# First expert layer of an attention and expert stack on rows sorted by expert

## The chip, the cores and the metric

The kernel runs on one core of a Trainium2 chip. The metric is the device time of one execution in microseconds (us). TensorE (PE) multiplies matrices; VectorE (DVE), ScalarE (ACT) and GpSimd (POOL) work on tiles in on-chip memory; SyncE (SP) issues transfers, and POOL issues the indirect ones, whose rows are named by a list. Each engine runs its own queue in order, and semaphores tie them together. TensorE runs at one of two clock levels, 1.2 or 2.4 GHz.

## What is computed

A residual stack of four pairs: attention over a context, then an expert layer (FFN), on x of 4 batches x 512 rows x 128 features. The change touches the first expert layer:

```python
gate_logits = x @ Wg + bg                                # x: 2048 rows, 8 experts
top_vals, top_idx = jax.lax.top_k(gate_logits, 2)
w = jax.nn.softmax(top_vals, axis=-1)
combine = jnp.sum(one_hot(top_idx, 8) * w[..., None], axis=-2)
h = jnp.einsum('td,edh->eth', xf, W0) + b0[:, None, :]    # 128 -> 512
g = silu(jnp.einsum('td,edh->eth', xf, W1) + b1[:, None, :])
y = jnp.einsum('eth,ehd->etd', h * g, W2) + b2[:, None, :]
out = jnp.einsum('te,etd->td', combine, y)
```

Two of the eight gates of a row are not zero. The second expert layer (one expert a row, with a capacity of 321 rows each) is computed in the kernel before on gathered rows already; the third and fourth (two experts a row) on all rows.

## The kernel before

Rows are held in four blocks of 512 (one batch each, B = 4), each of four tiles of 128 (TB = 4). x_tok has rows on partitions, xnT is the normalised x with features on partitions. Each engine has a hand-written program, `for s in range(N_SUB)`, over the eight sub-layers; the order in it is the order of the engine.

Sub-layer 0 is attention0. DVE's part of it calls replicate_columns, which waits until all of wP and woP (weights of the second attention, in_l1) have been loaded; SP issues these loads one after another behind its first loads. Then finish(0, b) adds the result of block b to x_tok, statistics and scale normalise it, and TensorE transposes the block.

Sub-layer 1 is ffn(0). It runs over expert e and block b, unit k = 4 e + b. hidden (TensorE) makes, for each of four chunks c of 128 hidden features, the products with W1 and W0 over 512 rows, and down the product with W2. A product is made of three matmuls (lines 2084 to 2086): weights and data are split into a high and a low part, in a format that needs one pass each, and high x high, high x low and low x high are summed. POOL makes the splits of the weights (w_p), ACT and DVE those of the hidden rows (h_p). ACT applies silu (gS), DVE multiplies with the other product (h_f), and sums y with the gate of each row, replicated over partitions through memory (gate_d, wrep). The result is summed in acc, transposed and added to x_tok by finish(1, b); the layer norm for the second attention follows, with key preparations (prep1) between.

POOL's before_heads(1), memsets and small splits for the second attention, stood behind that layer since its tiles share memory with it. routed() is the second expert layer: its products (lines 2569 and 2580) are single matmuls in fp32, and POOL stores and loads rows by indirect transfers (lines 802 and 809).

## Time and profile before

| | us |
|---|---|
| median of 3 runs (1529.68 to 1534.11) | 1530.49 |
| the profiled execution | 1535.88 |
| its span, first to last instruction | 1534.1 |
| mean granted clock of TensorE | 0.931 |
| busy: TensorE, DVE, ACT, POOL | 1333, 1115, 879, 685 |

The profile is of one execution. A row of the timeline has the start, the duration, the engine, the line of the kernel, the tiles written and read with their shapes, how many instructions are merged in it, and in brackets how long the engine was idle before it and what ended that. The page's tenths are shares of 40 equal slices of 38.4 us. TensorE's durations overlap; the time from start to start is what counts. An fp32 matmul appears as two instructions.

### The profile page before, as it was taken

Reading aid. Unit: us, or ns where it says so; the run is one execution under the profiler, and the core shown is the slowest. Engines: PE = TensorE matmul, PEld = TensorE weight load, DVE = VectorE, ACT = ScalarE, POOL = GpSimd, SP = SyncE. Lnnn points to the kernel's source line nnn. Section 1 sums busy time; section 2 is a strip of 40 time slices with the busy share of each in tenths; the row PEclk is TensorE's granted clock in tenths of the full one; section 3 lists DMA queues with packets and bytes.
Section 4 is the critical chain, followed back from the end, with each engine's and each line's share of the span. In section 5 each row is a group of like instructions: output and inputs, shape, how many; then the busy total and the mean of one; then the engine's idle time right before and its main releaser. Section 6 shows DMA issues by size and latency. Waiting matters only on the chain.

```text
span 1534.1 us, 23669 instructions
## 1 busy us (share of the span) xinstructions
PE 1333.4 (87%) x7106; PEld 975.5 (64%) x7106; DVE 1114.5 (73%) x2762; ACT 878.9 (57%) x2592; POOL 684.6 (45%) x1144
## 2 busy tenths in 40 slices
PE   4595989999967889779199999879789999998998
PEld 4432767888854555468177776556577776676886
DVE  4047778888887887842676667889866676788987
ACT  1001656556537889524187787534467878665664
POOL 2002322223025666434465556446355557545652
PEclk9657999999989999969599999999989999999999
DMA  3500014111042000222100000042101000014110
GB/s 79 21 22 0 22 38 150 55 49 35 1 50 62 1 2 2 58 81 70 48 12 18 1 2 8 5 148 97 34 15 43 1 2 14 1 29 144 62 56 28
DMA packets 85021, 60.17 MB, mean 39 GB/s; under 512 B 29779, under 2 KB 67691, under 8 KB 84896
## 3 DMA queue, kind: packets, MB, share of 16 engines
q1 hardware_dynamic: 83488, 55.97, 14.1%
q0 software_dynamic: 1408, 2.70, 0.6%
q8 instruction: 58, 0.95, 0.3%
q14 instruction: 67, 0.55, 0.1%
HBM read 52.38 MB, written 6.27 MB: 38 GB/s over the span
## 4 chain that ended last, share of the span: by engine, by line
PE 57%; DVE 17%; issue 6%; ACT 5%; POOL 4%; DMA 2%; SPq 0%; DVEq 0%; ACTq 0%; POOLq 0%
PE ps L2084 13%; PE ps L2085 12%; PE ps L2086 12%; PE ps L2221 5%; PE ps L2235 4%; DVE h_p L1753 4%; PE ps L2249 2%; ACT ex L1184 2%; DVE xn_tok L1383 2%; DVE acc L1772 1%; PE ps L2580 1%; PE ps L2569 1%; POOL pp L883 1%; DVE ln_st L1369 1%; PE ps L2170 1%
## 5 line engine op out<-in xcount | busy, mean ns | idle before, releaser
L883 POOL TENSOR_TENSOR pp<-ex,rc 128x256 f32<-128x256 f32 x384 | 235.8, 614 | 216.5 <-DVE rc L1799 155.0
L1753 DVE TENSOR_TENSOR h_p<-h_f,h_p 128x512 fp32r<-128x512 f32 x320 | 259.8, 835 | 29.1 <-POOL h_p L696 24.3
L1039 ACT ACTIVATE ex<-ps,nmx 128x154 f32<-128x154 f32 x512 | 194.3, 389 | 74.9 <-DVE nmx L1794 73.4
L1794 DVE TENSOR_REDUCE nmx<-ps 128x2 f32<-128x308 f32 x256 | 120.1, 471 | 93.1 <-PE ps L2086 92.9
L2084 PE MATMUL ps<-q_s,w_p 128*128 128x512 f32 x448 | 180.5, 403 | 7.5 <-DVE h_f L1978 3.0
L2086 PE MATMUL ps<-q_s,w_p 128*128 128x512 f32 x448 | 177.8, 397 | 0.0
L2085 PE MATMUL ps<-q_s,w_p 128*128 128x512 f32 x448 | 177.8, 397 | 0.0
L2084 PE MATMUL ps<-h_p,w_p 128*128 128x512 f32 x320 | 131.3, 410 | 14.4 <-DVE h_p L1753 12.9
L967 ACT ACTIVATE gS<-ps,biasT 128x512 f32<-128x512 f32 x128 | 88.2, 690 | 88.0 <-PE ps L2086 88.0
L696 POOL CAST h_p<-h_f 128x512 fp32r<-128x512 f32 x96 | 80.9, 843 | 118.3 <-ACT h_f L977 117.9
L1978 DVE SCALAR_TENSOR_TENSOR h_f<-ps,biasT,gS 128x512 f32<-128x512 f32 x128 | 95.6, 749 | 48.6 <-ACT gS L967 30.4
L2085 PE MATMUL ps<-h_p,w_p 128*128 128x512 f32 x320 | 127.5, 398 | 0.0
L2086 PE MATMUL ps<-h_p,w_p 128*128 128x512 f32 x320 | 126.9, 396 | 0.0
L654 POOL TENSOR_TENSOR ln_r<-ln_v,mhalf 128x4 f32<-128x4 f32 x36 | 38.2, 1062 | 195.4 <-DVE ln_v L1374 195.3
L674 POOL TENSOR_TENSOR w_p<-w_s,ones 128x512 fp32r<-128x512 f32 (+1 forms) x56 | 59.4, 1084 | 144.2 <-PE ps L2086 143.4
L2221 PEld LDWEIGHTS ps<-ident,pp 128*128 128x128 f32 x640 | 73.6, 141 | 59.8 <-POOL pp L884 34.2
L1184 ACT ACTIVATE ex<-ps,nmx 128x154 f32<-128x154 f32 x256 | 97.8, 394 | 20.5 <-DVE nmx L1647 20.1
L2084 PEld LDWEIGHTS ps<-q_s,w_p 128*128 128x128 f32 x448 | 84.8, 189 | 33.5 <-DVE h_f L1978 5.5
L884 POOL TENSOR_TENSOR pp<-ex,rc 128x52 f32<-128x52 f32 x384 | 105.1, 274 | 0.0
L2221 PE MATMUL ps<-ident,pp 128*128 128x128 f32 x640 | 99.5, 279 | 4.6 <-POOL pp L884 4.6
L1039 ACT ACTIVATION_READ_ACCUMULATOR ex<-ps,nmx 128x1 f32 x512 | 103.0, 201 | 0.0
L2084 PE MATMUL ps<-kp,q_s 128*128 128x308 f32 x256 | 95.7, 374 | 6.1 <-ACT ex L1039 6.1
(313 smaller groups left out, 3339.9 us busy)
## 6 DMA issues: line engine op xcount, KB each, us to landing
w_s<-in_L_ffn_W SPq DMA_DIRECT2D x48, 256.0 KB, 4.1
wrep<-gate_d SPq DMA_DIRECT2D x48, 256.0 KB, 3.5
xnT<-gate_d SPq DMA_DIRECT2D x48, 256.0 KB, 4.2
w_e<-in_L_ffn_W SPq DMA_DIRECT2D x8, 256.0 KB, 4.8
...
```

The source lines that it names most:

```text
L883: pool.tensor_tensor(pp[st % 2][:, m % 4, 2 * j:2 * j + 2, :], w[:, :, 0:P], r.broadcast_to([P, 2, P]), ALU.mult)
L884: pool.tensor_tensor(pp[st % 2][:, m % 4, 4, :].rearrange("p (h c) -> p h c", h=4)[:, 2 * j:2 * j + 2, 0:SK - P], w[:, :, P:SK], r.broadca ...
L967: act.activation(gS[c % 2][:, :], ps[:, c % 2, :], f["act"], **bias).then_inc(f_a, 1)
L1039: ins = act.activation(ex[:, tt % NEX, j, :], ps[:, tt % 3, j * SK:(j + 1) * SK], ACT.Exp, bias=nmx8[:, tt % 8, j:j + 1], accum_out=sm8[:, ...
L1184: ins = act.activation(ex[:, tt % NEX, j, :], ps[:, tt % 3, j * SK:(j + 1) * SK], ACT.Exp, bias=nmx8[:, tt % 8, j:j + 1], accum_out=sm8[:, ...
L1753: dve.tensor_tensor(lo[:, c, :], h_f[:, (n * k + c) % NHF, :], hi[:, c, :].bitcast(F32), ALU.subtract).then_inc(f_hl, 1)
L1794: dve.tensor_reduce(nmx8[:, tt % 8, :], ps[:, tt % 3, 0:2 * SK].rearrange("p (h s) -> p h s", h=2), AX.X, ALU.max, negate=True).then_inc(n ...
L1978: dve.scalar_tensor_tensor(out=h_f[:, (n * k + c) % NHF, :], in0=ps[:, 2 + c % 2, :], scalar=biasT[:, 32 + e * n + c:33 + e * n + c], in1= ...
L2084: mm(bank, w[0], x[0], start=first, stop=False)
L2085: mm(bank, w[0], x[1], start=False, stop=False)
L2086: return mm(bank, w[1], x[0], start=False, stop=last)
L2221: last = pe.transpose(ps[:, bank, k * P:(k + 1) * P], pp[st % 2][:, k, c, :], ident[:, :])
```

## The change

The first expert layer is no longer computed for all rows and experts. sorted_runs(), a program for each engine, does this:

1. TensorE computes the gate logits (choices), DVE picks the two experts of each row (choose), and triangular products (rank) give each of the 4096 choices its place among those of its expert (ranks).
2. runs_of_experts gives each expert whole runs of 256 places; (4096 + 8 x 255) / 256 gives 23 runs, always all computed. DVE (contents) and ACT (places) make two tables for each block, and 32 matmuls (lists) of them give, for each place of each run, the source row src_i, the row dst_i for its result, and its gate w_r.
3. For each run k: POOL gathers 2 x 128 rows of the normalised x from memory (xr_d); TensorE transposes them (columns), ACT copies them (xc_r). SP reads the run's expert from a table in on-chip memory (value_load) and loads its W1, W0 and W2 (three buffers). hidden_run makes 8 products of 256 columns, in fp32, ACT the silu with the expert's bias, DVE the product (products), down_run 8 products of 128 columns, DVE multiplies with the gate (weigh), and POOL scatters the rows into yr_d, one half for a row's first choice, one for its second, places without a row behind both.
4. The bias b2 comes from four matmuls with the gates (turn, bias_out) in runs 1 to 5. When the last scatters have landed, SP loads both halves of yr_d into acc and y_second, and finish(1, b) adds both.

before_heads(1) now stands on POOL behind the first four gathers. Its place and the tables' sit in memory that the splits used; the splits, gate replication and sums of this layer are gone. The stores that fill xs_d and y_d for the second expert layer come behind the loads of yr_d. Layers 2 to 4 keep their computation.

```diff
-    DENSE = (0, 2, 3)
-    CNT = (0, 1, 1, 2, 3)
+    DENSE = (2, 3)
+    CNT = (0, 0, 0, 1, 2)
+    SPARSE = 0
+    HALVES = 2
+    RUN = HALVES * P
+    NRUN = (2 * B * S + E * (RUN - 1)) // RUN
+    NCOL = NRUN * HALVES
+    NXG, NW = 4, 3
...
+            sp.dma_start(b1_rows[:, :], t["L0_ffn_b1"]).then_inc(in_l1, 16)
+            sp.dma_start(b0_rows[:, :], t["L0_ffn_b0"]).then_inc(in_l1, 16)
+            sp.wait_ge(const_g, 4)
+            for k in range(TB):
+                sp.dma_start(b2_blk[k * E:(k + 1) * E, k * D:(k + 1) * D], t["L0_ffn_b2"]).then_inc(in_l1, 16)
...
+                def first_weights(k):
+                    u = k % NW
+                    e = sp.value_load(expert_i[0:1, k:k + 1], min_val=0, max_val=E - 1)
+                    wait(sp, s_h, 2 * (k - NW + 1))
+                    sp.dma_start(w1_r[u][:, :], t[f["w1"]][bass.ds(e, 1)].rearrange("a p h -> p (a h)")).then_inc(s_wr[u], 16)
+                    sp.dma_start(w0_r[u][:, :], t[f["w0"]][bass.ds(e, 1)].rearrange("a p h -> p (a h)")).then_inc(s_wr[u], 16)
+                    return e
+                def last_weights(k, e):
+                    u = k % NW
+                    wait(sp, s_yp, k - NW + 1)
+                    sp.dma_start(w2_r[u][:, :, :], t[f["w2"]][bass.ds(e, 1)].rearrange("a (c p) d -> p (a c) d", p=P)).then_inc(s_wr[u], 16)
+                for b in range(B):
+                    sp.wait_ge(ln_ok, B * ln_index(1) + b + 1)
+                    sp.dma_start(xr_d[b * S:(b + 1) * S, :].rearrange("(k p) d -> p k d", p=P), xn_tok[:, tiles(b), :]).then_inc(s_xd, 16)
+                sp.wait_ge(*by_v("expert"))
+                for k in range(NRUN):
+                    e = first_weights(k)
+                    last_weights(k, e)
+                for u in range(2):
+                    sp.wait_ge(s_out[u], 16 * HALVES * ((NRUN + 1 - u) // 2))
+                for b in range(B):
+                    for c, into in enumerate((acc, y_second)):
+                        sp.dma_start(into[:, bsl(b)].rearrange("p (k d) -> p k d", k=TB),
+                                     yr_d[c * B * S + b * S:c * B * S + (b + 1) * S, :].rearrange("(k p) d -> p k d", p=P)).then_inc(y_in[b], 16)
...
-            dense(0)
+            sorted_runs()
...
+                def gather(k):
+                    wait(pool, s_xp, k - NXG + 1)
+                    for h in range(HALVES):
+                        c = k * HALVES + h
+                        pool.indirect_dma_start(xr[k % NXG][:, h, :], None, xr_d[:, :], bass.IndirectOffsetOnAxis(ap=src_i[:, c:c + 1], axis=0)).then_inc(s_xr[k % NXG], 16)
+                def scatter(k):
+                    pool.wait_ge(s_y, k + 1)
+                    for h in range(HALVES):
+                        c = k * HALVES + h
+                        pool.indirect_dma_start(yr_d[:, :], bass.IndirectOffsetOnAxis(ap=dst_i[:, c:c + 1], axis=0), yr[k % 2][:, h, :], None).then_inc(s_out[k % 2], 16)
+                pool.wait_ge(*by_v("ids"))
+                pool.wait_ge(s_xd, 16 * B)
+                for k in range(NXG):
+                    gather(k)
+                before_heads(1)
+                for k in range(NRUN):
+                    scatter(k)
+                    if k + NXG < NRUN:
+                        gather(k + NXG)
...
+                act.preload_act_table(FFN[SPARSE]["act"])
+                act.wait_ge(*by_p("bias"))
+                act.activation(bias_r[:, :, :], ps[:, 7, 0:8 * NRUN].rearrange("p (c k) -> p c k", c=8), ACT.Identity).then_inc(s_a, 1)
+                act.wait_ge(*by_a("bias"))
+                columns(0)
+                columns(1)
+                for k in range(NRUN):
+                    gates(k, 0)
+                    gates(k, 1)
+                    if k + 2 < NRUN:
+                        columns(k + 2)
+                    if 1 <= k <= B:
+                        turned(k - 1)
...
+                    dve.wait_ge(y_in[b], 32)
+                    link(dve.tensor_tensor(x_tok[:, tiles(b), :], x_tok[:, tiles(b), :], y_second[:, bsl(b)].rearrange("p (n d) -> p n d", n=TB), ALU.add))
+                    more = acc[:, bsl(b)]
...
+                def contents(b):
+                    def over_cols(ap):
+                        return ap.rearrange("p (n a) -> p n a", a=1)
+                    into = what[b // 2][:, b % 2, :, :]
+                    link(dve.tensor_tensor(same[:, :, :], col_of[:, :].rearrange("p (a k) -> p a k", a=1).broadcast_to([P, 2 * TB, NCOL]),
+                                           over_cols(first[:, b, :]).broadcast_to([P, 2 * TB, NCOL]), ALU.is_equal))
+                    for c in range(2):
+                        dve.tensor_tensor(into[:, c * TB:(c + 1) * TB, NCOL:2 * NCOL], same[:, c * TB:(c + 1) * TB, :], over_cols(r_w[:, c, tiles(b)]).broadcast_to([P, TB, NCOL]), ALU.mult)
+                    link(dve.tensor_tensor(into[:, :, 0:NCOL], same[:, :, :], over_cols(val[:, b, :]).broadcast_to([P, 2 * TB, NCOL]), ALU.mult))
+                    dve.sem_inc(s_v, 1)
...
+                def products(k, q):
+                    G = 2 * k + q
+                    dve.wait_ge(s_ga, G + 1)
+                    dve.wait_ge(s_h, G + 1)
+                    wait(dve, s_yp, k - 1)
+                    for c in range(2):
+                        ins = dve.scalar_tensor_tensor(out=h_r[k % 2][:, 2 * q + c, :], in0=ps[:, 2 + G % 2, c * RUN:(c + 1) * RUN], scalar=bias_r[:, 4 + 2 * q + c, k:k + 1],
+                                                       in1=g_r[G % 2][:, c, :], op0=ALU.add, op1=ALU.mult)
+                    ins.then_inc(s_hd, 1)
+                def weigh(k):
+                    dve.wait_ge(s_yp, k + 1)
+                    wait(dve, s_out[k % 2], 16 * HALVES * (k // 2))
+                    for h in range(HALVES):
+                        ins = dve.tensor_scalar(yr[k % 2][:, h, :], ps[:, 5, h * D:(h + 1) * D], w_r[:, HALVES * k + h:HALVES * k + h + 1], None, ALU.mult)
+                    ins.then_inc(s_y, 1)
+                def add_bias(b):
+                    dve.wait_ge(*by_p("b2", b))
+                    dve.tensor_tensor(x_tok[:, tiles(b), :], x_tok[:, tiles(b), :], ps[:, 7, :].rearrange("p (n d) -> p n d", n=TB), ALU.add).then_inc(s_v, 1)
...
+                def hidden_run(k):
+                    pe.wait_ge(s_wr[k % NW], 48 * (k // NW + 1))
+                    pe.wait_ge(s_x, k + 1)
+                    for q in range(2):
+                        G = 2 * k + q
+                        wait(pe, s_ga, G - 1)
+                        for c in range(2):
+                            last = mm(ps[:, G % 2, c * RUN:(c + 1) * RUN], w1_r[k % NW][:, (2 * q + c) * P:(2 * q + c + 1) * P], xc_r[k % 2][:, :], start=True, stop=True)
+                        last.then_inc(s_g, 1)
+                        wait(pe, s_hd, G - 1)
+                        for c in range(2):
+                            last = mm(ps[:, 2 + G % 2, c * RUN:(c + 1) * RUN], w0_r[k % NW][:, (2 * q + c) * P:(2 * q + c + 1) * P], xc_r[k % 2][:, :], start=True, stop=True)
+                        last.then_inc(s_h, 1)
+                def down_run(k):
+                    pe.wait_ge(s_hd, 2 * k + 2)
+                    wait(pe, s_y, k)
+                    for h in range(HALVES):
+                        for c in range(4):
+                            last = mm(ps[:, 5, h * D:(h + 1) * D], h_r[k % 2][:, c, h * P:(h + 1) * P], w2_r[k % NW][:, c, :], start=(c == 0), stop=(c == 3))
+                    last.then_inc(s_yp, 1)
...
+                hidden_run(0)
+                for k in range(NRUN):
+                    if k + 1 < NRUN:
+                        hidden_run(k + 1)
+                    if k + 2 < NRUN:
+                        columns(k + 2)
+                    down_run(k)
+                    if 1 <= k <= B:
+                        turn(k - 1)
+                    if 2 <= k < 2 + B:
+                        bias_out(k - 2)
```

The order of TensorE at the start of the layer, before: transposes of attention 0's result (acc) and of the normalised x (xn_tok), then the split matmuls; w_p_67, w_p_68 are the parts of W1, w_p_75, w_p_76 those of W0, q_s holds those of x.

```order
L2053 MATMUL ps<-ident,acc 128x128 x16
L2040 MATMUL ps<-ident,xn_tok 128x128 x16
L2084 MATMUL ps<-q_s,w_p_67 128x512
L2085 MATMUL ps<-q_s,w_p_67 128x512
L2086 MATMUL ps<-q_s,w_p_68 128x512
L2084 MATMUL ps<-q_s,w_p_75 128x512
L2085 MATMUL ps<-q_s,w_p_75 128x512
L2086 MATMUL ps<-q_s,w_p_76 128x512
```

Six matmuls make one pair of hidden products there, and they start right behind the transposes.

TensorE now, from the count of choices per expert (total) on: biases, the first half of the lists, then the columns of runs 0 and 1 (xr), the hidden products of run 0, and further down columns(2) and down_run(0).

```order
L3140 MATMUL ps<-total,ones 128x8
L3076 MATMUL ps<-expert_oh,b_rows 128x23 x8
L3067 MATMUL ps<-what_177,where 128x92 x16
...
L3084 MATMUL ps<-ident,xr_148 128x128 x2
L3084 MATMUL ps<-ident,xr_149 128x128 x2
L3095 MATMUL ps<-xc_r_167,w_r_154 128x256 x2
L3099 MATMUL ps<-xc_r_167,w_r_157 128x256 x2
...
L3084 MATMUL ps<-ident,xr_150 128x128 x2
L3108 MATMUL ps<-w_r_160,h_r_163 128x128 x8
```

Between the transposes and the first product stand the gate logits, ranks, biases and lists; the columns of a run stand two runs ahead of it, behind the hidden products of the next run.

POOL before, behind the layer norms' ln_r: the splits of the first expert's weights (w_s) and of x.

```order
L654 TENSOR_TENSOR ln_r<-ln_v,mhalf 128x4 x8
L674 TENSOR_TENSOR w_p_67<-w_s,ones 128x512
L674 TENSOR_TENSOR w_p_71<-w_s,ones 128x512
L674 TENSOR_TENSOR w_p_75<-w_s_79,ones 128x512
L681 TENSOR_TENSOR w_p_68<-w_s,w_p_67 128x512
L681 TENSOR_TENSOR w_p_72<-w_s,w_p_71 128x512
L681 TENSOR_TENSOR w_p_76<-w_s_79,w_p_75 128x512
L704 TENSOR_TENSOR q_s<-xnT,q_s 128x512 x4
```

These splits are gone from POOL.

POOL now: gathers of four runs, before_heads (its last op is the memset of wkT), then scatter and gather in turn.

```order
L778 TENSOR_TENSOR ln_r<-ln_v,mhalf 128x4 x8
L909 DMA xr_148<-xr_d,src_i 128x128 x2
L909 DMA xr_149<-xr_d,src_i 128x128 x2
...
L909 DMA xr_151<-xr_d,src_i 128x128 x2
L985 MEMSET kz_111 128x2464
L986 MEMSET pp_104 128x4x128
...
L1001 MEMSET wkT_99 128x512
L916 DMA yr_d<-yr_152,dst_i 9984x128 x2
L909 DMA xr_148<-xr_d,src_i 128x128 x2
L916 DMA yr_d<-yr_153,dst_i 9984x128 x2
L909 DMA xr_149<-xr_d,src_i 128x128 x2
```

The gather of run k + 4 stands behind the scatter of run k, and before_heads ahead of the first scatter.

SP at the start of the program, before: biases and mask, then the weights of the second attention, and the first expert's weights.

```order
L498 DMA bias_rows<-in_L_ffn_b 32x128 x4
L499 DMA mask_i<-in_mask_Bx1xSxS_if 128x16x154
L505 DMA wP<-in_L_xattn_Wq 8x8x1 x16
L505 DMA wP<-in_L_xattn_Wk 8x8x1 x16
L505 DMA wP<-in_L_xattn_Wv 8x8x1 x16
L509 DMA woP<-in_L_xattn_Wo 8x128x1 x16
L540 DMA w_s<-in_L_ffn_W 128x512
```

The loads of w_s went at this place with their addresses fixed.

SP now, the same place, and then the start of sorted_runs: stores of the normalised rows, the read of the expert of run 0, and its first two loads (the third, of W2, follows).

```order
L580 DMA mask_i<-in_mask_Bx1xSxS_if 128x16x154
L582 DMA b_rows<-in_L_ffn_b 8x512
L583 DMA b_rows<-in_L_ffn_b 8x512
L586 DMA b_blk<-in_L_ffn_b 8x128 x4
L591 DMA wP<-in_L_xattn_Wq 8x8x1 x16
...
L595 DMA woP<-in_L_xattn_Wo 8x128x1 x16
L682 DMA xr_d<-xn_tok 128x4x128 x4
L668 TENSOR_LOAD expert_i
L668 ISA x2
L670 ISA
L670 DMA w_r_154<-in_L_ffn_W 128x512
L671 DMA w_r_157<-in_L_ffn_W 128x512
```

Six loads stand ahead of wP and woP, and the loads of expert weights stand behind a read of expert_i.

## Rows read from the trace of the kernel before

**Rows 1.** The page, parts 1 and 2: busy time, and clock in 40 slices.

```profile
PE 1333.4 (87%) x7106; PEld 975.5 (64%) x7106; DVE 1114.5 (73%) x2762; ACT 878.9 (57%) x2592; POOL 684.6 (45%) x1144
...
PEclk9657999999989999969599999999989999999999
```

**Rows 2.** Windows: length, busy of PE, PEld, DVE, ACT, POOL, clock, DMA, GB/s.

```profile
154.70:440.30 285.60, 277.95 (x1192) 222.53 (x1192) 234.79 (x401) 165.12 (x270) 65.96 (x49) 0.98 0.15 47
```

**Rows 3.** Timeline, TensorE: start, duration, line; the layer's first matmuls and late ones.

```profile
154.69 0.77 PE L2084 MATMUL ps<-q_s,w_p 128*128 128x512 f32 x1 [2.72 <-ACT q_s L914]
...
158.67 0.52 PE L2084 MATMUL ps<-q_s,w_p 128*128 128x512 f32 x1
...
430.65 0.39 PE L2085 MATMUL ps<-q_s,w_p 128*128 128x512 f32 x1
430.88 0.39 PE L2086 MATMUL ps<-q_s,w_p 128*128 128x512 f32 x1
```

**Rows 4.** Timeline, TensorE in the middle (fp32) expert layer.

```profile
691.71 2.87 PE L2580 MATMUL ps<-w_s,h_s 128*128 128x128 f32 x24
694.42 2.33 PE L2569 MATMUL ps<-xs,w_e 128*128 128x321 f32 x8
696.58 0.44 PE L2557 MATMUL ps<-ident,xg 128*128 128x128 f32 x3
696.86 2.87 PE L2580 MATMUL ps<-w_s,h_s 128*128 128x128 f32 x24
```

**Rows 5.** Timeline, ACT in the same layer: four activations of 321 columns.

```profile
697.40 1.78 ACT L1245 ACTIVATE h_s<-ps,biasT 128x321 f32<-128x321 f32 x4
```

**Rows 6.** Timeline, DVE and POOL at that layer's end: PSUM operand, indirect stores.

```profile
727.86 0.42 DVE L1600 TENSOR_TENSOR y_s<-ps,b2rep 128x256 f32<-128x256 f32 x1 [1.38 <-PE ps L2580]
728.04 0.96 POOL L809 DMA_INDIRECT y_d<-y_s,xg  x1 [0.30 <-issue]
...
729.31 0.91 POOL L809 DMA_INDIRECT y_d<-y_s,xg  x1 [0.30 <-issue]
...
733.08 0.92 POOL L809 DMA_INDIRECT y_d<-y_s,xg  x1 [0.30 <-issue]
```

**Rows 7.** DMA issues: count, KB each, median us from issue to landing.

```profile
w_e<-in_L_ffn_W SPq DMA_DIRECT2D x8, 256.0 KB, 4.8
...
y_d<-y_s,xg POOLq DMA_INDIRECT x24, 2.2
```

**Rows 8.** DMA rate in 40 slices of the stretch 686 to 706 us.

```profile
GB/s 286 272 307 327 312 343 337 341 335 328 338 257 71 5 0 0 0 0 0 119 217 359 311 174 0 0 131 0 94 94 135 338 330 222 46 19 131 0 46 21
```

**Rows 9.** Chain of work: start, duration, four 128x8 products of the gate (x8).

```profile
654.38 1.86 PE ps L2537 x8
```

**Rows 10.** Timeline, DVE: first and last op of the choice for one block.

```profile
648.06 0.18 DVE L1555 COPY lg<-ps 128x32 f32<-128x32 f32 x1
...
650.13 0.17 DVE L1572 TENSOR_TENSOR cum<-cum,oh_sum 128x8 f32<-128x8 f32 x1
```

**Rows 11.** Timeline, DVE: scaling of block 3 before the first expert layer.

```profile
146.49 4.31 DVE L1383 TENSOR_SCALAR xn_tok<-x_tok,ln_mv,ln_r 128x128 f32<-128x128 f32 x4 [0.20 <-POOL ln_r L654]
```

**Rows 12.** Timeline, SP's loads at the start, and DVE behind the last.

```profile
11.46 1.70 SPq L498 DMA_DIRECT2D bias_rows<-in_L_ffn_b  x4
...
34.49 35.98 SPq L509 DMA_DIRECT2D woP<-in_L_xattn_Wo  x16
...
76.22 0.90 DVE L1450 COPY wP<-wP 128x128 f32<-128x128 f32 x6 [32.26 <-DMA woP<-in_L_xattn_Wo]
```

**Rows 13.** Timeline, DVE behind the first and behind the middle expert layer.

```profile
440.27 0.68 DVE L1414 TENSOR_TENSOR x_tok<-x_tok,ps 128x512 f32<-128x512 f32 x1
...
445.71 2.17 DVE L1624 SCALAR_TENSOR_TENSOR kz<-kz_hi,neg_lo,ps 32x308 fp32r<-32x308 f32 x4 [3.12 <-POOL pp L846]
...
461.48 1.11 DVE L1383 TENSOR_SCALAR xn_tok<-x_tok,ln_mv,ln_r 128x128 f32<-128x128 f32 x4
...
738.25 0.69 DVE L1414 TENSOR_TENSOR x_tok<-x_tok,acc 128x512 f32<-128x512 f32 x1 [9.11 <-DMA acc<-y_d]
```

554 lines of the change are left out of this document (379 added, 175 removed).

## The prediction

> **What bounds the kernel now.** I read first the page's busy line and clock row [rows 1]: TensorE is busy 87% of the span, mostly at full clock. Then the stretch from the first matmul of the first expert layer, at 154.7 us, to its end at 440.3 us, when the sum of row block 0 is added to x_tok [rows 2, 3, 13]. In these 285.6 us TensorE is busy 278 us. The layer makes 8 experts x 4 row blocks x 36 matmuls = 1152 (12 hidden products, three matmuls each), one every 0.235 us at full clock [rows 3], 271 us. So TensorE bounds this stage, and every row goes through all eight experts although two of them have a weight. A cut of its work pays, until another chain ends later.
>
> **Removed.** These 285.6 us. The splits of weights and x on POOL, the replication of gates and the sums of y go too; they lay beside TensorE and count nothing.
>
> **Added 1: SP's queue at the start.** Six loads (two of b1_rows and b0_rows, four of b2_blk) stand ahead of the loads of wP and woP. SP issues small loads 0.43 us each, about 0.47 us apart [rows 12], and the woP loads end at 70.5 us. DVE waited 32.3 us for just those, and the chain of attention 0 waits for DVE behind it [rows 12]. So all that follows is later by 6 x 0.47 = 2.8 us.
>
> **Added 2: routing.** I walked DVE and TensorE through the new order from 134.4 us on (x_tok of block 0; this part stands as before). Prices: a group of 128x8 products, four matmuls, takes TensorE 1.86 us at the low clock of that stretch, 0.46 us a matmul [rows 1, 9]. What choose(b) does for one block on DVE took 2.2 us, with some ten small ops about 0.2 us apart [rows 10]; it now has three more ops, so 2.6 us. ranks(b) is six small ops, 1.4 us. TensorE has, per block, choices(b) 1.9 us and rank(b), five matmuls, 2.3 us, in one line with the transposes of the next block, which wait for DVE. So the two engines wait for each other in turn:
> - choose(0) 146.1 to 148.7, scale of block 2 to 152.0, transposes, rank(0) and choices(1) on TensorE to 157.2 (DVE idles 5 us), choose(1) to 159.9, scale of block 3 and ranks(0) to 162.5, choose(2) after choices(2), 166.4 to 169.0, choose(3) to 173.0, ranks(3) to 177.1.
> - runs_of_experts, 14 small ops, to 180.6, shares to 180.9. contents(b): 368 elements take about 0.54 us, half of them 0.35 us (estimates from the 128x256 op at 0.42 us [rows 6] and the small ones [rows 10]), so 0.54 + 2 x 0.35 + 0.54 with gaps 1.95 us, four times: 188.7.
> - The list matmuls follow DVE; those of the last block take 2 us if the clock has risen by then (biases and lists keep TensorE busy from 179 on), up to 3.7 us if not: 190.7. dst_i and src_i: 191.2.
> - POOL issues two gathers 1.27 us apart [rows 6] per run, and PE turns runs 0 and 1 before the first product: the fourth gather starts at 195.1 and lands 2.2 us later [rows 7]. First hidden product at 198, against 154.7: **43.3 us**. The expert weights are asked for from 179 on, 19 us ahead, and cost nothing here; ACT's squares end about 181.
>
> **Added 3: 23 runs.** Of these products the fp32 layer in the middle of the kernel has rows: four matmuls of 321 columns from start to start 2.16 us, so 0.54 us each, linear in columns (0.43 us for 256); twelve of 128 columns 2.71 us, 0.226 us each; three transposes 0.28 us [rows 4]. A run has 8 of 256 columns (3.45), 8 of 128 (1.81), 2 transposes (0.19): 5.45 us, 23 of them 125.3 us, less 0.4 us for the two transposes counted above. ACT: one copy and four 128x256 gates, 0.39 us each from 0.445 at 321 [rows 5], 2.0 us. DVE: four ops at 0.42 us and two smaller, 2.3 us. POOL: two scatters, two gathers, 5.05 us [rows 6]. None exceeds TensorE alone, but POOL is close.
> - In the four runs with turn(b) and bias_out(b), ACT waits at turned(b) for a transpose behind down_run, and its next gates come 1.2 us late; bias_out has 512 columns, 0.87 us; with the turn 2.2 us a run, **8.9 us**.
> - TensorE idles before the first run, so the first 4 us run at half clock, as at 154.7 where nine matmuls took 4.0 us instead of 2.1 [rows 3]: 2 us.
> - The ring of rows: columns(k) turned, hidden products, weigh about 3.75 us after columns(k+2), two scatters and one gather ahead (3 x 1.27), second gather landing after L, transposes 0.2. This closes over two runs: period = 3.9 + L/2. TensorE's 5.45 holds up to L = 3.1 us. The bounds for L are the 2.2 us of a scatter and the 4.8 us of a 256 KB load beside others [rows 7]. I take the middle, 3.5 us, since a gather reads from memory while loads run: 5.65 us, 0.20 x 23 = **5 us**.
> - w2 of run k is issued after down_run(k-3): period = (5.45 + landing)/2, 5.1 us with 4.8 us for the landing [rows 7]; slack.
> - Bytes: 768 KB of weights and 256 KB of rows a run; at the 330 GB/s that the busiest slices moved [rows 8] 3.2 us of 5.65.
>
> Sum: 124.9 + 8.9 + 2 + 5 = **141 us**.
>
> **Added 4: the way back.** weigh 0.5, second scatter 1.3 behind the first. In the middle layer the first x_tok addition came 5.2 us after the last scatter began [rows 6, 13]; here block 0 needs two loads: 5.7. **7.5 us**. What follows (layer norm, key preparations) took DVE 22.3 us to 462.6 with 3.1 us of waiting for POOL's memsets [rows 13]. These now stand after gather(3), hidden behind runs 0 and 1 (5.3 us to the last memset); four second additions of 0.72 us take their place: 0.2 us less, taken as 0. If their cover is gone, 5.3 us.
>
> **Sum.** 285.6 - 43.3 - 141 - 7.5 - 2.8 = 91 us. The profiled execution had a span of 1534.1 and a time of 1535.9, so 1445 on its scale; it lies 5.4 us above the median of 1530.5, and against the median it is **1439 us**. Layers behind are unchanged; their initial stores of xs_d and y_d slide with the layer and have the whole of attention 1.
>
> **A rule against this change.** The row: DVE's four scalings of block 3 took 4.31 us [rows 11] while POOL split weights, where the same four take 1.11 beside an idle POOL [rows 13]; so the two do block each other. POOL's indirect stores beside DVE's ops on PSUM took 0.96 us and alone 0.92 [rows 6]. The Trainium skill, SBUF — State Buffer, "SBUF: two separate sides", says that transfers issued by GpSimd starve while VectorE holds the shared port, 620 ns becoming about 3100. By that rule the four of a run would take some 12 us and the kernel would lose; by the row they don't. The same rule spares VectorE ops with a PSUM operand, and all in the runs have one: by that rule, the trace agrees.
>
> **Rivals.**
> - *A transfer chain sets the run.* L near 4.8 us gives 6.3 us, or w2's landing stretched to 7 us by the other two loads and the rows gives 6.2; for it speaks that all four kinds of transfer run at once, and that the layer has only three weight buffers; against it the 3.2 of 5.65 us. 0.6 x 23 = 14 us more: 1453.
> - *Routing longer.* If the clock stays low and each small op costs 0.05 us more (some 120 in a row), 10 us more: 1449.
> - *Slower than before: POOL's issue.* If DVE holds back each indirect transfer, the period is four issues. From 2.4 us each (9.6 us a run = 5.65 + 91/23) nothing is gained; with the factor 3.9 of [rows 11] on 1.27 us it is 4.9 us, 19.6 us a run, +320 us: about 1760. Against it [rows 6].
> - *It doesn't do what it says.* The number of runs is fixed at 23 and nothing is skipped; were all fp32 products double the rows' price, +120 us, 1559. [Rows 4] exclude it nearly.
>
> **How the numbers follow.** Forecast 60%, transfer chain 22%, routing longer 13%, POOL's issue 3%, price of products 1%, something between 1%. Low end: period 5.45 (-5) and routing 12 us shorter, if DVE and TensorE interleave better: 1422. High end: transfer chain and routing longer, 1439 + 14 + 10 + 3 for the memsets: 1466. About 0.3% is what a measurement of this kernel can tell from no change. Faster 0.95, same 0.01, slower 0.04.
>
> **What would show it.** TensorE's first 256-column product about 201 us (2.8 us shift in it), start to start of runs 5.4 to 5.7 us late in the stage, PE busy over 90% there, the granted clock full; about 347 us for the first addition of y_second. Wrong: idle TensorE before the transposes with the gather as releaser (ring), before the first product of a run with a weight load as releaser (w2), POOL's indirect rows over 2 us, or a routing over 50 us.

## The result, and the profile after

The changed kernel takes **1438.2 us** (median of 4 runs, 1434.3 to 1441.4) against 1530.1 us (4 runs, 1529.5 to 1534.1): ratio 0.939, 95% interval 0.936 to 0.942. The forecast was 1439. The profiled execution took 1436.3 us, its span 1434.6. Busy times and clock row of its page, to be read beside [rows 1]:

```profile
PE 1225.5 (85%) x6850; PEld 903.5 (63%) x6850; DVE 957.1 (67%) x2652; ACT 772.0 (54%) x2480; POOL 701.7 (49%) x1189
PEclk9667579997799996886999999999899999999999
```

108 us of TensorE's busy time are gone. In slice 5 (143 to 179 us) the clock row has 5: there the routing lies. Next come two windows, the end of the routing and the 23 runs, with the columns of [rows 2]:

```profile
160.00:193.00 33.00, 21.80 (x99) 20.93 (x98) 15.31 (x67) 12.36 (x30) 4.99 (x5) 0.50 0.26 80
193.70:334.00 140.30, 134.89 (x793) 116.78 (x793) 52.28 (x141) 44.60 (x119) 89.90 (x96) 0.99 0.51 152
```

In the runs TensorE is busy 134.9 of 140.3 us at full clock, and the transfer engines half the time. The layer is still bound by TensorE. The next rows are the marks on DVE that end each stage, to be read beside [rows 12] and [rows 13]: the copy behind the woP loads, the addition of block 0 to x_tok, the list of places, the last weigh, the first addition of y_second, the last scale:

```profile
69.12 0.90 DVE L1633 COPY wP<-wP 128x128 f32<-128x128 f32 x6 [24.63 <-DMA woP<-in_L_xattn_Wo]
125.27 0.69 DVE L1597 TENSOR_TENSOR x_tok<-x_tok,ps 128x512 f32<-128x512 f32 x1 [4.28 <-PE ps L2378]
185.80 0.20 DVE L2249 TENSOR_TENSOR dst_i<-ps,spare_r 128x46 int32<-128x46 f32 x1 [8.82 <-PE ps L3067]
333.89 0.61 DVE L2276 TENSOR_SCALAR yr<-ps,w_r 128x128 f32<-128x128 f32 x2 [2.21 <-PE ps L3108]
342.19 0.69 DVE L1589 TENSOR_TENSOR x_tok<-x_tok,y_second 128x512 f32<-128x512 f32 x1 [7.69 <-DMA y_second<-yr_d]
363.01 1.11 DVE L1562 TENSOR_SCALAR xn_tok<-x_tok,ln_mv,ln_r 128x128 f32<-128x128 f32 x4
```

TensorE's timeline between them: the biases, the lists, the first two transposes, the first hidden products.

```profile
168.28 3.57 PE L3076 MATMUL ps<-expert_oh,b_rows 8*128 8x23 f32 x16 [3.21 <-DVE expert_oh L2216]
171.83 13.93 PE L3067 MATMUL ps<-what,where 128*128 128x92 f32 x64
190.61 0.69 PE L3084 MATMUL ps<-ident,xr 128*128 128x128 f32 x2 [4.84 <-DMA xr<-xr_d,src_i]
193.18 0.69 PE L3084 MATMUL ps<-ident,xr 128*128 128x128 f32 x2 [1.89 <-DMA xr<-xr_d,src_i]
193.66 1.91 PE L3095 MATMUL ps<-xc_r,w_r 128*128 128x256 f32 x4
195.37 1.91 PE L3099 MATMUL ps<-xc_r,w_r 128*128 128x256 f32 x4
197.08 1.11 PE L3095 MATMUL ps<-xc_r,w_r 128*128 128x256 f32 x4
```

Both traces, stage by stage, beside the prediction:

| stage | before, us | after, us | predicted |
|---|---|---|---|
| first addition to x_tok | 134.42 | 125.27 | 137.2 |
| from there to the first hidden product (before: of the old layer) | 20.3 | 68.4 | 63.6 |
| the layer itself; the 23 runs to the last weigh | 285.6 | 140.2 | 141 |
| last weigh to the first addition of y_second | | 8.3 | 7.5 |
| from the layer's first addition to the end of the span | 1093.8 | 1092.4 | same |

The right end holds to 0.1%, but three terms do not: the start came 9.2 us earlier where 2.8 later was forecast, the routing is 4.8 us longer, and 0.8 us change sides between runs and way back. Against the profile of before the forecast was 1445 and the profiled run took 1436.3; against the median the difference is 0.8 us. The experiments ask what lies behind the start, the runs, the routing and the covers.

### The profile page after: what moved, and what is told of

It is laid out like the page before. It is cut to its first block, busy times and chain, and to the rows that moved or that the text cites. A ratio compares the mean times of both kernels' runs of the same rounds, so it can differ in the third digit from the quotient of the medians.

```text
span 1434.6 us, 23042 instructions
## 1 busy us (share of the span) xinstructions
PE 1225.5 (85%) x6850; PEld 903.5 (63%) x6850; DVE 957.1 (67%) x2652; ACT 772.0 (54%) x2480; POOL 701.7 (49%) x1189
## 4 chain that ended last, share of the span: by engine, by line
PE 55%; DVE 18%; issue 9%; POOL 5%; DMA 5%; ACT 5%; SPq 4%; DVEq 0%; ACTq 0%; POOLq 0%
PE ps L2409 8%; PE ps L2411 7%; PE ps L2410 7%; PE ps L2533 5%; PE ps L2547 4%; DVE h_p L1933 3%; PE ps L2561 2%; DMA xr<-xr_d,src_i 2%; PE ps L3108 2%; SPq L595 2%; DVE xn_tok L1562 2%; ACT ex L1310 2%; PE ps L3095 2%; DVE ln_st L1548 2%; PE ps L2879 1%
## 5 line engine op out<-in xcount | busy, mean ns | idle before, releaser
L1933 DVE TENSOR_TENSOR h_p<-h_f,h_p 128x512 fp32r<-128x512 f32 x192 | 160.5, 871 | 25.4 <-POOL h_p L819 22.8
L2409 PE MATMUL ps<-kp,q_s 128*128 128x308 f32 x256 | 94.8, 370 | 6.6 <-ACT ex L1165 6.6
L2267 DVE SCALAR_TENSOR_TENSOR h_r<-ps,bias_r,g_r 128x256 f32<-128x256 f32 x92 | 38.3, 477 | 91.6 <-ACT g_r L1466 81.2
L2409 PE MATMUL ps<-h_p,w_p 128*128 128x512 f32 x192 | 80.2, 418 | 14.5 <-DVE h_p L1933 12.8
L1106 ACT ACTIVATE h_f<-ps,biasT 128x512 f32<-128x512 f32 x128 | 82.0, 695 | 9.4 <-DVE h_p L1933 9.4
L2365 PE MATMUL ps<-ident,xn_tok 128*128 128x128 f32 x80 | 20.9, 412 | 69.3 <-DVE xn_tok L1562 68.9
L2409 PE MATMUL ps<-q_s,w_p 128*128 128x512 f32 x192 | 77.4, 403 | 1.6 <-POOL q_s L824 1.5
L2411 PE MATMUL ps<-kp,q_s 128*128 128x308 f32 x256 | 78.7, 308 | 0.0
L2410 PE MATMUL ps<-kp,q_s 128*128 128x308 f32 x256 | 78.7, 307 | 0.0
L2410 PE MATMUL ps<-h_p,w_p 128*128 128x512 f32 x192 | 76.6, 399 | 0.0
L2411 PE MATMUL ps<-h_p,w_p 128*128 128x512 f32 x192 | 76.3, 397 | 0.0
L2411 PE MATMUL ps<-q_s,w_p 128*128 128x512 f32 x192 | 76.2, 397 | 0.0
```

Source lines behind the costliest of these rows:

```text
L1106: act.activation(h_f[:, (n * k + c) % NHF, :], bank, f["act"], **bias).then_inc(f_a, 1)
L1933: dve.tensor_tensor(lo[:, c, :], h_f[:, (n * k + c) % NHF, :], hi[:, c, :].bitcast(F32), ALU.subtract).then_inc(f_hl, 1)
L2409: mm(bank, w[0], x[0], start=first, stop=False)
L2410: mm(bank, w[0], x[1], start=False, stop=False)
L2411: return mm(bank, w[1], x[0], start=False, stop=last)
```

## Experiments

The ratio and its 95% interval are against the kernel before, run on the same chip. The intervals of the changed kernels overlap in most cases, so a difference of a few us between two of them is called shown only where a trace shows it too.

**The six loads at the start.** One kernel changes the changed kernel, two the kernel before.

```diff
# loads_apart: the loads of b1_rows, b0_rows, b2_blk behind those of woP
-            sp.dma_start(b1_rows[:, :], t["L0_ffn_b1"]).then_inc(in_l1, 16)
...
+            sp.dma_start(b1_rows[:, :], t["L0_ffn_b1"]).then_inc(in_b, 16)
...
-                pe.wait_ge(in_l1, 16 * (3 * HEADS + 16 + 2 + TB))
+                pe.wait_ge(in_b, 16 * (2 + TB))
```

> The changed kernel, with the six loads of b1, b0 and b2 issued behind the loads of woP, on a semaphore of their own that only the bias products wait for. Theory of the prediction (each load ahead costs its issue, 0.47 us): 2.8 us faster than the changed kernel. Rival, from the traces (x_tok of block 0 came 9.1 us earlier in the changed kernel although six loads stand ahead): the six loads ahead are what made the strided loads behind them go faster; then this kernel is slower by about 6 us than the changed one.

Measured: 1442.0 us (1434.3 to 1445.8), ratio 0.939 (0.935 to 0.944). The interval holds that of the changed kernel, so neither 2.8 us less nor 6 us more is shown.

```diff
# b_six: the kernel before with six such loads ahead of those of wP
+            sp.dma_start(pt_s[0][0:E, :], t["L0_ffn_b1"]).then_inc(in_l1, 16)
+            sp.dma_start(pt_s[1][0:E, :], t["L0_ffn_b0"]).then_inc(in_l1, 16)
+            for k in range(TB):
+                sp.dma_start(pt_s[2][k * E:(k + 1) * E, k * D:(k + 1) * D], t["L0_ffn_b2"]).then_inc(in_l1, 16)
...
```

> The kernel before, with the six loads of the changed kernel added at the same place of SyncE's queue, into tiles that are free then. Theory of the prediction: 2.8 us slower than before. Rival (their place shifts the strided loads onto a faster pattern, 29.6 instead of 36.0 us for woP): 3 to 7 us faster than before. Third possibility: the strided loads vary from execution to execution by themselves; then neither sign is clear of the spread.

Measured: 1531.1 us (1526.2 to 1539.4, 10 runs), ratio 0.999 (0.997 to 1.001).

```diff
# b_experts_wait: the kernel before, loads of expert weights wait for those of woP
+            sp.wait_ge(in_l1, 16 * (3 * HEADS + 16))
```

> The kernel before, with SyncE waiting until all loads of wP and woP have landed before it issues the first expert loads. Theory (in the kernel before, 1.5 MB of expert loads right behind woP delayed its landing: 5.8 us from the last issue to VectorE's start, 4.0 us in the changed kernel): VectorE starts about 1.7 us earlier and the kernel is 1 to 2 us faster; the expert weights arrive 6 us later and are still in time. Rival (the difference lies in the issue of the strided loads alone): no change.

Measured: 1534.1 us (1523.7 to 1542.4, 10 runs), ratio 1.001 (0.997 to 1.005).

SP's rows of the woP loads (start, duration of the issue) in the traces of the kernel after, loads_apart, b_experts_wait and b_six, in this order:

```profile
35.48 29.60 SPq L595 DMA_DIRECT2D woP<-in_L_xattn_Wo  x16
```
```profile
35.05 33.97 SPq L591 DMA_DIRECT2D woP<-in_L_xattn_Wo  x16
```
```profile
34.23 39.26 SPq L509 DMA_DIRECT2D woP<-in_L_xattn_Wo  x16
```
```profile
34.74 30.48 SPq L513 DMA_DIRECT2D woP<-in_L_xattn_Wo  x16
```

The same 16 loads take 29.6 to 39.3 us in these traces, and 36.0 in that of the kernel before [rows 12]. Over all fourteen kernels of this document, ten of the eleven with six loads ahead took 29.1 to 31.0 us and one (loads_twice) 36.6; the three without took 34.0, 36.0 and 39.3. But in the times of ten runs b_six differs from the kernel before by 0.1%, and its interval leaves room for 4.6 us gained or 2.1 us lost, not for the 2.8 us of the prediction. In b_experts_wait DVE still starts 5.3 us behind the last issue (5.8 in the kernel before), so the expert loads were not what made the woP loads land late. Of the 9 us between the starts of the kernels before and after, the six loads can have given at most those 4.6; the rest is, as far as the runs show, a difference of two executions. Whether six loads ahead shorten the issue stays open: the traces lean to it, the times do not show it.

**Gathers first.** The ring of rows was a term of the sum (5 us): the gather of run k + 4 waits on POOL behind the two scatters of run k, and TensorE meets its rows two runs later.

```diff
                 for k in range(NRUN):
-                    scatter(k)
                     if k + NXG < NRUN:
                         gather(k + NXG)
+                    scatter(k)
```

> The changed kernel with one edit on GpSimd: the gather of run k+4 is issued ahead of the scatter of run k. Theory (ring of rows: period 3.9 + L/2 with the two scatters in it): the gather then waits only for its buffer, which is free a run earlier; all transposes find their rows, every run takes 5.45 us instead of the 5.7 us measured late in the stage, and the time falls by 4 to 6 us. Rival (weight loads, or memory traffic as such, stretch the runs): the idle time before the transposes moves to the first hidden product of a run and the time falls by less than 1.5 us.

Measured: 1434.8 us (1433.5 to 1438.2), ratio 0.936 (0.933 to 0.939). In the kernel after the late transposes wait for their rows, first block; with the gathers first they don't, second block (TensorE, one late run each):

```profile
269.93 1.03 PE L3099 MATMUL ps<-xc_r,w_r 128*128 128x256 f32 x4
271.56 0.44 PE L3084 MATMUL ps<-ident,xr 128*128 128x128 f32 x2 [0.61 <-DMA xr<-xr_d,src_i]
271.83 1.95 PE L3108 MATMUL ps<-w_r,h_r 128*128 128x128 f32 x16
```
```profile
276.22 1.03 PE L3099 MATMUL ps<-xc_r,w_r 128*128 128x256 f32 x4
277.09 0.38 PE L3084 MATMUL ps<-ident,xr 128*128 128x128 f32 x2
277.31 1.95 PE L3108 MATMUL ps<-w_r,h_r 128*128 128x128 f32 x16
```

Thirteen late runs (down_run to down_run, from the eighth on) take 5.46 us each where the kernel after has 5.46 to 6.59, 5.81 in the mean. 5.46 is TensorE's own time, forecast as 5.45. The gathers still land after 3.0 us (median from 215 to 320 us), but they are asked for a run earlier. From the first to the last down_run it is 124.5 us against 129.3: the ring cost 4.8 us, forecast 5. The medians differ by 3.4 us, but the intervals of the two ratios overlap; the trace shows it, the times only agree.

**Who stretches the gathers, and how much room the transfers have.** loads_small (the kernel after) and loads_twice (gathers first):

```diff
# loads_small: from run 3 on a sliver of each weight
+                    n = 4 * P if k < NW else 16
-                    sp.dma_start(w1_r[u][:, :], t[f["w1"]][bass.ds(e, 1)].rearrange("a p h -> p (a h)")).then_inc(s_wr[u], 16)
+                    sp.dma_start(w1_r[u][:, 0:n], t[f["w1"]][bass.ds(e, 1), :, 0:n].rearrange("a p h -> p (a h)")).then_inc(s_wr[u], 16)
...
# loads_twice: each weight once more, into tiles that are free in these runs
+                    for w1_to, w0_to in ((w1_r[u], w0_r[u]), (more_r[u][0], more_r[u][1])):
...
-                    pe.wait_ge(s_wr[k % NW], 48 * (k // NW + 1))
+                    pe.wait_ge(s_wr[k % NW], 96 * (k // NW + 1))
```

> The changed kernel, except that from run 3 on each load of an expert's weights brings only a sliver (64 bytes a partition, some 24 KB a run in place of 768 KB); the products are then made with the weights of runs 0 to 2 that lie in the buffers, so the sum of the layer is another one. It asks whether the traffic of the weights sets the landing of the gathers and with it the period of the runs. In the changed kernel 13 late runs took 5.81 us each, the gathers landed after 3.0 us (median) and the transposes waited for them. Theory A (the ring of rows is made of POOL's order and of POOL's issue, 1.29 us each): the landing falls to 2.2 to 2.6 us, but the period stays between 5.6 and 5.8 us; time 0 to 4 us less than the changed kernel's 1438. Theory B (the weights' transfers stretch the gathers): the landing falls to about 2.2 us and all late runs take 5.46 us, TensorE's own time; 7 to 8 us less, about 1430. Theory C (the wait is for the weights themselves): the period falls to 5.46 and the landing of the gathers stays at 3.0.

> The kernel with the gathers issued ahead of the scatters (runs 5.46 us each, set by TensorE, 1434.8 us), with every weight load of the 23 runs issued a second time into tiles that are free then; hidden_run waits for all six. A run then moves 1536 KB of weights and 256 KB of rows instead of 1024 KB. It prices the slack of the transfers. My theory, after the prediction's account (3.2 of 5.65 us are needed at 330 GB/s; period by w2's ring (5.45 + landing)/2): 1.79 MB at 330 GB/s are 5.4 us, just at TensorE's 5.46, and landings grow to 5 to 7 us, so a run takes 5.5 to 6.2 us: 0 to 17 us more, middle 1442. Rival (the transfer chain was close to being the bound already): a run takes 7 us or more, +35 us, 1470. Other rival (the transfers have far more slack than the bytes say): 5.46 us as before, 1435, and the slices of the stage show over 330 GB/s.

Measured: loads_small 1434.2 us (1431.5 to 1437.4), ratio 0.938 (0.934 to 0.941); loads_twice 1439.0 us (1435.7 to 1442.8), ratio 0.940 (0.936 to 0.943). DMA part of the traces from 215 to 320 us, busy tenths, rates, then the issues with count, KB each and median us to landing; loads_small first:

```profile
DMA packets 9845, 5.39 MB, mean 51 GB/s; under 512 B 8690, under 2 KB 8690, under 8 KB 9836
xr<-xr_d,src_i POOLq DMA_INDIRECT x36, 2.5
```
```profile
DMA  9999797995985899999999999999999999999999
DMA packets 31164, 32.75 MB, mean 312 GB/s; under 512 B 2850, under 2 KB 20867, under 8 KB 31155
more_r<-in_L_ffn_W SPq DMA_DIRECT2D x54, 256.0 KB, 4.5
xr<-xr_d,src_i POOLq DMA_INDIRECT x36, 4.2
```

The kernel after shows 3.0 us there. With slivers the gathers land in 2.5 us and the late runs take 5.47 us although POOL's order is the old one: theory B, though its 7 to 8 us was too much. From the first to the last down_run it is 124.5 us against 129.3, as with the gathers first, and the median is 4.0 us lower. So the old order costs time only where the weights' traffic delays the gathers. The Trainium skill (DMA: Bandwidth & Descriptors, Anatomy of one DMA — SWDGE (gpsimd) path) gives a transfer of 64 KB issued by GpSimd about 2.15 us, an estimate from its formula; the trace comes near it only with the other traffic nearly gone, and beside it measures 3.0 and 4.2. With the doubled loads the transfer engines are busy 96% at 312 GB/s and the gathers take 4.2 us, and still the late runs take 5.52: gathers issued a run earlier have the room for that. So TensorE stays the bound at 1.75 times the bytes, which agrees with the prediction's account (3.2 of 5.65 us). From first hidden product to last down_run it is 0.6 us more than with single loads; the other 3.6 us of the median are not shown by this stage, and the intervals overlap.

**Run size.** This kernel has the gathers first too.

```diff
-    HALVES = 2
+    HALVES = 1
```

> The kernel with the gathers issued ahead of the scatters, with runs of 128 rows: 39 runs in place of 23 (4992 rows computed in place of 5888). By TensorE a run then takes 8 x 0.226 for the hidden products, 4 x 0.226 for W2 and 0.09 for the transpose, 2.8 us; 39 of them 109 us, against 125.6. But each run loads its 768 KB of weights, and 128 KB move in and out. Theory A (my account of the transfers): 896 KB at 330 GB/s are 2.7 us, just below TensorE, but the ring of w2 gives (2.8 + landing) / 2 with a landing of 4.5 us, as in the kernel with doubled loads, so 3.6 us a run: 142 us, 14 us more than now (1449), with TensorE waiting for weights. Rival B (TensorE stays the bound): 2.8 us a run, 16 us less: 1419. Rival C (POOL's issue, two transfers of 1.29 us a run, or SP's three loads with the reading of the expert's number): 2.6 us, below TensorE, unless SP takes over 0.9 us a load.

Measured: 1440.6 us (1436.2 to 1445.3), ratio 0.943 (0.937 to 0.949). TensorE's waits of the stretch, and one of them in its timeline:

```profile
PE ps L3095 <- DMA w_r<-in_L_ffn_W: 13.1, 17, 1.5
PE ps L3095 <- ACT g_r L1466: 1.4, 2, 0.9
```
```profile
244.82 0.71 PE L3095 MATMUL ps<-xc_r,w_r 128*128 128x128 f32 x4 [0.85 <-DMA w_r<-in_L_ffn_W]
```

A run takes 3.24 us where nothing waits, not 2.8: the four products with W2 take 1.14 us until the next run starts instead of 0.90, and each of the first two pairs of hidden products 0.50 to 0.55 instead of 0.45. That each now waits for a neighbour which 256 columns had covered is likely, but not shown. Thirteen late runs take 3.65 us in the mean, since the weights come late 17 times in the 39 runs, 13.1 us in all. From the first hidden product to the last down_run it is 141.5 us against 133.7: what the 15% fewer rows save is more than lost. That is theory A, whose 142 us was right. Its "14 us more" was not, since it counted from 125.6 us, the bare price of 23 runs, and not from the 133.7 that they take with their biases and the first run's clock; the median is 5.8 us above that of the kernel with the gathers first.

**The cover of the memsets.**

```diff
-                before_heads(1)
                 for k in range(NRUN):
...
                     scatter(k)
+                before_heads(1)
```

> The kernel with the gathers ahead of the scatters, and before_heads(1) on POOL moved from behind the first four gathers to behind the last scatter, its cover gone. The prediction said: 5.3 us if that cover is gone. Theory A (as the prediction): +5.3 us, 1440. Theory B (from the trace of the kernel with the gathers first): POOL's last scatter is issued at 334.2 and its next work, the first reciprocal root of the layer norm, comes at 342.3; the memsets take 7.4 us (198.3 to 205.6) and end at 341.6, before anything waits for them: +0 to 1 us, 1435. And the second run may start up to 1 us earlier, since scatter 0 and gather 4 no longer stand behind the memsets.

Measured: 1436.4 us (1434.0 to 1439.8), ratio 0.939 (0.935 to 0.943). POOL, last memset:

```profile
339.96 0.97 POOL L1001 MEMSET wkT<- 128x512 f32 x2
```

They run from 332.9 to 340.9 us. DVE waits for the rows of yr_d until 338.1, and POOL is needed next at 341.2, for the layer norm, so they end just in time; the first addition of y_second comes 8.3 us behind the last weigh in both kernels and the last scale 20.9 us behind that (20.8 with the memsets early). Theory B: it costs nothing, and the prediction's "if their cover is gone, 5.3 us" was wrong. The way back is itself a cover, with 0.3 us to spare.

**The clock of the lists.** Two sizes of one edit; the results of the matmuls added are read by nobody.

```diff
# warm, with the gathers first; lists_mixed has also the last two lines
+                spin(16)
                 biases()
                 lists()
+                spin(22)
                 columns(0)
+                spin(8)
                 columns(1)
...
+                    for _ in range(n):
+                        mm(ps[:, 3, 0:256], ident_bf[:, :], ident[:, :].bitcast(BF16), start=True, stop=True)
...
+                            if b < 2:
+                                mm(ps[:, 3, 0:256], ident_bf[:, :], ident[:, :].bitcast(BF16), start=True, stop=True)
```

> The kernel with the gathers ahead of the scatters, with matmuls that nobody reads (256 columns, bf16) in TensorE's idle time: 16 before the biases (3.2 us idle there), 22 between lists and the first transposes (4.75 us idle), 8 between the transposes of runs 0 and 1 (1.8 us idle). It asks what the low clock of the lists and of the first run costs. There the 64 instructions of the lists took 13.93 us at the low clock, although TensorE had been busy without a gap for 17.5 us by their end; the first products of 256 columns ran 3.4 us at the low clock. Theory A (activity ahead raises the clock and the small matmuls keep it): lists take about 7 to 8 us, the first hidden product comes 5 to 6 us earlier, and the first run gains 1.7 us: 7 us less than 1434.8, 1428. Theory B (the wide matmuls raise the clock, the narrow ones of the lists let it fall again or keep it low): lists about 14 us still, the first run at full clock: 1.7 us less, 1433. Theory C (no effect at all, the clock stays low until 197): 1435.

> The kernel with matmuls that nobody reads in TensorE's idle time (before the biases, behind the lists, between the first transposes; there the lists still took 13.96 us at the low clock, and the clock rose 2 us into the matmuls behind them), and 16 more of them among the lists, one of 256 columns behind each of the first 16 of the 32 products. At the low clock one costs 0.22 us (3.57 us for 16). Theory A (it is the narrow fp32 products that keep the clock low, wide ones between them raise it): the granted clock rises within the lists; up to the rise the stretch takes some 0.65 us for a product and a wide one, then half, and lists and wide ones end after about 11 us, 3 us before; 1429. Theory B (they don't raise it): lists take 13.9 + 3.5 = 17.4 us, 3.5 us more than the kernel without, and the first hidden product comes 3.5 us later: about 1436 against 1432.

Measured: warm 1432.3 us (1429.2 to 1438.0), ratio 0.937 (0.933 to 0.941); lists_mixed 1429.3 us (1422.7 to 1434.2), ratio 0.935 (0.930 to 0.941). TensorE in warm, then in lists_mixed (its rows in the lists alternate, four stand for them):

```profile
162.34 3.57 PE L3129 MATMUL ps<-ident,ident_bf 128*128 128x256 bf16 x16
169.38 13.96 PE L3067 MATMUL ps<-what,where 128*128 128x92 f32 x64
183.13 3.51 PE L3129 MATMUL ps<-ident,ident_bf 128*128 128x256 bf16 x22
191.03 1.03 PE L3095 MATMUL ps<-xc_r,w_r 128*128 128x256 f32 x4
```
```profile
161.31 3.14 PE L3131 MATMUL ps<-ident,ident_bf 128*128 128x256 bf16 x16
164.66 1.93 PE L3078 MATMUL ps<-expert_oh,b_rows 8*128 8x23 f32 x16 [0.21 <-DVE expert_oh L2216]
168.21 0.71 PE L3067 MATMUL ps<-what,where 128*128 128x92 f32 x2 [1.62 <-DVEq L2244]
...
173.35 0.42 PE L3069 MATMUL ps<-ident,ident_bf 128*128 128x256 bf16 x1
...
174.43 0.36 PE L3067 MATMUL ps<-what,where 128*128 128x92 f32 x2
...
175.94 3.71 PE L3067 MATMUL ps<-what,where 128*128 128x92 f32 x32
```

In warm the 16 wide matmuls ahead don't raise the clock and the lists run at 1.2 GHz to their end, although TensorE has not paused since 162; behind them it rises, and the first run is at 2.4 GHz. From first hidden product to last down_run it is 131.6 us against 133.7: 2.1 us for the first run, forecast 2. In lists_mixed the same 16 matmuls ahead did raise it: the granted clock is 1.00 from 164 to 167 us, and the biases take 1.93 us instead of 3.60. TensorE then idled 1.62 us, and from 168 us the clock was 0.50 again, so the lists began at the low level there too. Between their products wide matmuls stand, and the clock rises 5.7 us into the lists, in best, below, 4.9 us into them. The 16 products left take 3.6 us where 7.0 is their price at the low level. In the traces without them the lists ran at the low level to their end. From the first addition to the first hidden product it is 65.8 us in place of 68.2. So the price of the lists is the clock's. What in the added matmuls raised it (their width, their type or their mere number) is not shown.

**Two steps late, and all together.** late has the gathers first and these two; best has them with all of lists_mixed.

```diff
                 batch_maximum(B - 1)
-                replicate_columns()
...
                 lists()
                 combine()
+                replicate_columns()
...
-                    if 1 <= k <= B:
-                        turned(k - 1)
+                    if 2 <= k < 2 + B:
+                        turned(k - 2)
```

> The kernel with the gathers ahead of the scatters (1434.8 us) and two steps moved. (1) DVE's replicate_columns, which waits for all loads of wP and woP, from the middle of attention 0 to behind combine(), where DVE waits 10 us for the first products. (2) ACT's turned(b) one run later, behind the gates that TensorE waits for. For (1): TensorE idled 4.8 us for hc behind replicate_columns (66.7 to 71.5). Theory A: hc comes as soon as its sums are there, the addition of block 0 to x_tok comes 4.8 us earlier, near 122, and no longer moves with the woP loads; 1430. Rival: DVE's later steps wait for something else that came at the same time, 0 us. For (2): five runs took 6.97 us in place of 5.46, of which 1.1 us are bias_out and the turn; the wait for the gates goes and leaves 6.5 us each, 0.5 x 5 = 2.5 us less. Rival: the turned copy then holds TensorE's bias_out instead, 6.97 stay. Together 7 us less, 1427.

Measured: 1427.4 us (1422.8 to 1427.5), ratio 0.932 (0.927 to 0.938), 7.4 us below the kernel with the gathers first, forecast 7, though the intervals still overlap. DVE has its tile hc at 61.16 us and not at 71.33, and TensorE goes on earlier:

```profile
67.43 3.75 PE L3015 MATMUL ps<-prob,ctx_tok 77*128 77x512 f32 x4 [1.51 <-ACT prob L1422]
```

It stood at 71.54 behind an idle 4.80 us for hc with the gathers first. Now it waits 1.5 us for ACT's probabilities, so 3.3 of the 4.8 us are won. The first addition to x_tok comes at 121.86 us, near the 122 forecast, but that proves little: in warm, lists_mixed and halves1, which lack this edit, it comes at 122.69, 121.66 and 122.25, with a granted clock of 0.79 to 0.80 from 70 to 125 us where the kernel with the gathers first had 0.72. The five runs with turned copies and biases take 32.7 us where they took 34.6: 1.9 us, not 2.5, since only the first of them, which has no bias_out, falls to 5.57, and the others to 6.82. bias_out itself costs 1.1 us.

> All that the runs so far found, together: the gathers ahead of the scatters, replicate_columns and turned(b) late, and matmuls that nobody reads before the biases, among the first 16 products of the lists, behind the lists and between the first transposes. Theory A (the gains add): the kernel with the two late steps measured 1427.4; the wide matmuls take 2.4 us from the routing (from the addition of block 0 to the first hidden product 65.8 us in place of 68.2) and 2.1 us from the first run: 1423, 15 us below the changed kernel, and the routing from the first addition to the first hidden product takes 65 to 67 us in its trace. Theory B (the earlier start changes what the clock does, and the wide matmuls cost their 3.5 us without raising it in the lists): the stretch takes 70 to 72 us, first run still at full clock: 1428.

Measured: **1424.4 us** (1418.2 to 1427.3, 6 runs), ratio 0.931 (0.927 to 0.935), 13.8 us below the changed kernel's median, and the fastest here. Its interval lies below that of the changed kernel (0.936 to 0.942); against late they overlap. Theory A: from the first addition (120.58) to the first hidden product (185.93) 65.4 us. But the clock fell again in the last idle time before the first run, which it was not to do:

```profile
185.93 1.92 PE L3097 MATMUL ps<-xc_r,w_r 128*128 128x256 f32 x4
187.64 1.87 PE L3101 MATMUL ps<-xc_r,w_r 128*128 128x256 f32 x4
189.34 1.03 PE L3097 MATMUL ps<-xc_r,w_r 128*128 128x256 f32 x4
```

These two rows cost 1.7 us of the 2.1 hoped for.

## Why the prediction was right, point by point

- **Bound and removal.** Right: TensorE bounded the layer, and nothing that lay beside it took its place. 285.6 us went. (The 12 products of a unit are eight hidden ones and four with W2; the count of 36 matmuls stands.)
- **Added 1, the loads.** Wrong: the step "all that follows is later by 6 x 0.47 = 2.8 us" took the 36 us of the woP loads as fixed. They are 29.1 to 39.3 us from trace to trace, and b_six excludes a cost above 2.1 us. The starts vary further by the clock: in the window of 70 to 125 us it was granted 0.66 before, 0.74 after and 0.80 in lists_mixed.
- **Added 2, routing.** 68.4 us for 63.6. DVE was quicker: contents(3) ended 51.7 us behind the first addition, forecast 54.3. The step that failed is "the list matmuls follow DVE; those of the last block take 2 us ..., up to 3.7 us if not". The lists start behind the biases at 171.8, one product takes 0.435 us, eight of them 3.5 us at the low level, while DVE makes a block's table in 1.8. So TensorE was the slower from the first block on, and 8.8 us of lists stood behind DVE's last table. Of the rival "routing longer" (+10 us) the low clock came true, the dearer small ops did not; lists_mixed shows that the clock is the cause.
- **Added 3, the runs.** 141 forecast, 140.2 measured. TensorE's 5.45 us a run is 5.46. The four turned and bias runs were to cost 8.9 us; five runs took 34.6 us (gathers first) for 27.3, so 7.3 us, as bias_out covers a part of the wait for the gates: without that wait, in late, a run with bias_out falls only from 6.97 to 6.82. The first run's clock 2 us, measured 2.1. The ring 5 us (0.20 x 23 is 4.6, rounded up), measured 4.8, the mechanism shown by gather_first. But its price was partly luck: by "3.9 + L/2" the median landing of 3.0 us would give 5.4, no loss, and the 3.5 us taken for L was too long. In the trace the 46 gathers landed after 2.4 to 4.5 us, so some are later than the 3.1 us at which the ring is even; that these made TensorE wait is likely, but was not matched run by run. Late runs took 5.46 to 6.59 us, 5.81 in the mean and above the 5.7 named as a sign, and TensorE did idle before the transposes.
- **w2 ring, bytes.** Right in that neither bounds a run, by loads_twice; the weights' median landing was 3.3 us, not 4.8.
- **Added 4, the way back.** 7.5 forecast, 8.3 measured; the two loads landed 0.8 us later than the estimate from one. What follows: 0 forecast, 0.4 us less from first addition to the end of the last scale (21.9 for 22.3). The price of a lost cover was wrong.
- **A rule against the change.** POOL's indirect transfers took 0.97 us (gathers, median) and 0.98 us (scatters) beside DVE in the runs, 1.20 at most, and 1.29 us from start to start, close to [rows 6] (0.91 to 0.96 and 1.27):

```profile
271.94 0.98 POOL L909 DMA_INDIRECT xr<-xr_d,src_i  x1 [0.31 <-issue]
273.23 0.97 POOL L909 DMA_INDIRECT xr<-xr_d,src_i  x1 [0.30 <-issue]
```

  The rival of 1760 us is out. The Trainium skill, SBUF — State Buffer, "SBUF: two separate sides", lets a DVE instruction with at most one operand in SBUF, outside its two-port modes, run without contention with GpSimd. The DVE ops of a run read their other operand from PSUM, and the trace agrees.
- **Rivals.** The transfer chain (+14 us) had the right place but not the size: the rows' ring, not the weights', and inside the forecast. With 128-row runs it is the weights that come late.
- **The sum.** On the profile's scale the forecast was 8.6 us too high: -12 for the start, +4.8 routing, -0.8 runs, +0.8 way back, -1.4 behind. Against the median the start drops out, since the trace of before had a late start and lay 5.4 us above its median. So the end is right to 1 us partly by errors that cancel: the routing, 4.8 too short, against the 2.8 of the loads and small ones. A hit within 1 us, where runs of one kernel spread over 7 us and more, is luck; that the large terms were right is not.
